# Unread products ahead of 15 waits of a decoder's middle stage, with new lane orders

## The chip, the cores and the metric

The kernel runs on one core of one Trainium2 chip. The metric is the device time of one execution in microseconds; three executions of the kernel before were timed. One further execution was profiled. Engines are named as in the profile: PE (TensorE), DVE (VectorE), ACT (ScalarE), POOL (GpSimd), SP (SyncE).

## The reference, cut to what matters

The reference is a decoder of four layers on x of 16 x 256 tokens of width 128, each layer an attention, a cross attention and a feed-forward part, each with a residual and a layer norm. The middle stage of the kernel computes the last of these of layer 0 (the quantised feed-forward's down projection and its norm), then layer 1's segment attention, cross attention and the gate of its experts:

```python
x = _layernorm(x + _L0_ffn_ref(x, ...))          # lead lane: down projection, norm
x = _layernorm(x + _L1_attn_ref(x, ...))         # near lane
x = _layernorm(x + _L1_xattn_ref(x, ctx_1024, ...))   # far lane
x = _layernorm(x + _L1_ffn_ref(x, ...))          # far lane: gate; then the experts
...
# _L1_attn_ref: 16 heads of 8, segments of 64 tokens
out = _attn(q, k, v)                             # inside the segment
kd = k[:, :, :, dil_idx, :]                      # every 4th key
for off in range(1, NN + 1):                     # two neighbours on each side
    for sign in (-1, 1):
        cross = _attn(q, kd[:, nc], vd[:, nc])
        out = out + jnp.where(valid, cross * w, 0.0)
return out @ Wo + bo
```

The last stage computes layers 2 and 3 from the gated convolution on.

## The kernel before

The 4096 tokens are worked on in eight groups of 512 (`ITERS` = 8), features on the 128 partitions. The program runs stages one after the other: the first stage (layer 0's recurrence and cross attention), the quantised up projection, the middle stage, the choice and the experts of layer 1, the ends, the convolution, and the last stage.

**Lanes.** Each stage is written as lanes: Python generators, one for each engine, that issue a step's instructions and then yield. The middle stage has three. *Lead* (`LaneDown`, then a `LaneNorm`) takes group it+1, *near* (`LaneSegment`, then a `LaneNorm`) takes group it, *far* (`LaneWide`, `LaneNorm`, `LaneGate`) takes group it-1. Near uses one half of PSUM (four banks), lead and far share the other half, one after the other. `middle` runs lead for group 0 alone, then near 0 with lead 1 (`ORDERS["alone"]`), then six steady rounds (`ORDERS["middle"]`: near against far followed by lead), then near 7 with far 6 (`ORDERS["closing"]`), then far 7 alone.

**What sets the order.** `turns` goes through a string for each engine: at "n" it takes the next step of the near lane, at "f" of the other. So a string fixes the order of instructions in an engine's queue; engines execute their queues in order, and semaphores (`wait_ge`, `then_inc`) tie them to each other. The last stage has two equal lanes with strings of its own for its four rounds.

**The near lane's steps on PE** (`LaneSegment.pe`): the projections q, k, v (L1181 to L1191); for each half b of the group the local part: scores (L1208), peaks (transposes of the maxima, L1168), turned (L1222), out in two halves (L1233), back (L1244); then for each half the dilated part: dil_scores (L1257), dil_peaks (L1168), dil_turned (L1270), dil_out (L1279), dil_sum (L920 and L1292); then the output products z (L920 and L939) and the norm's transposes (L1021). Between them DVE searches the maxima (L1368, L1388), makes the query (L1340) and normalises (L1378 to L1407), and ACT takes the exponentials (L1318, L1328). The norm: DVE statistics (L991, L996), POOL's reciprocal root (L1007, L1009), DVE scaling (L1000), PE transposes (L1021), ACT copies (L1032). The lead lane quantises on DVE (L210 to L214) before its product (L1127). The far lane: q (L1454), k and v (L1464), folded output weights (L1477), scores (L1485, L1489), transposes first and second (L1514), out (L920, L1522), gate (L1638).

**Unread products.** `keep_busy(pe, bank, place)` issues as many products of the 128 x 128 identity with itself as `BUSY` names for the place, into a bank whose contents nobody reads any more; for a place that `BUSY` doesn't name it issues nothing. Before the change `BUSY` names only places of the choice and of the experts, whose products are L2801 in the profile. `LaneSegment.pause` calls it for the near lane with a bank of the other lane while that lane's flag `beside["free"]` is set; none of its places is in `BUSY`.

Of the kernel before, what the change touches and what calls it, by code (L numbers as in the profile page):

```python
# [27 lines left out]
P = 128  # L28
# [696 lines left out]
class Convolution:  # L725
# [54 lines left out]
    def dve(self, dve, n):  # L780
        m, i = self.mem, n % 4
        dve.wait_ge(*self.sig.done("pe", f"c{n}", 0))
        if n >= 2:
# [9 lines left out]
BUSY = {'taken': 20, 'chosen': 5, 'choice start': 8, 'choice same': 4, 'choice bit': 3, 'choice rank': 40}  # L793
# [13 lines left out]
        "pe": "nffnnnnnfnnnnnnnnnffffnnnnnnnnnnnnnnnn",  # L807
        "dve": "fnnnfnnnnffffnnnnfnnnnnnnnnnnnnn",
        "act": "nnnnnnnnnnnnnnfffffnnnnnfnnnnn",
# [3 lines left out]
        "pe": "nffnfnfnfnnnfnfffnnfnnfnnffnfnnnfffffnnfffnfnnnfffnnnfnnnn",  # L813
        "dve": "nffnfnffnnnffnffnffnnnfnnffffffnnfffnnfnfffffnnnnnnn",
        "act": "nffffnnnnfffffnnnnnffffnnnnffffffnnnnnnnffffffnnfn",
# [3 lines left out]
        "pe": "nffnfnfnfnnnnfffnfnfnnfnfnfnfnnnnfffnffnnnnnnnnnnn",  # L819
        "dve": "nffnfnffnnnffnfnfffnnnfnnfffffnnfnnnfnnfnnnnn",  # L820
        "act": "fnfffnnnnfffffnnnnnffffnnnnnnffffnnnffnnnnn",
# [9 lines left out]
        "pe": "nnffnnnfnnnnnffffffnfnnfnnfnffnfnfnnnfnnffnffnffffnnnnnnnnnnffffnfffffffnnnnnnnnnfffnfffffffnnfnfnfnfnffnnfffffnfnnffnff"  # L831
             "nnnnfnnffnffnnfnfnnnnnnffnnfnnnffffffnfnfnnnfnfffnfnnfnnfnnfnfnfffffnnnnnnnffffnfffnfnfnfnfnfnfnfnfnfnfnfnfnfnfnfnfnfnfn"
             "fnfnfnnfnfnfnfnfnfnfnfnnffnnnnfnnnfnfffffffnnnnnnnnfnnnfffffffffffnnnnnnnnnnnnfffffnnnnnnnnnnfffnnnnffffffnfnfnffnnnfnnf"
             "nfnfnnnnnffffnffnfnffnfnnffnnfnnffnnnnfnnnfnnnnfffnnnnnnnnnfnfnnffnfnffnfnfnnnnfffnffffffffnnnfffffnfffnnfnnfnnnfnfffnfn"
             "nfffnnnnnnnfffnfnffnnfnffnfffnnnnnnfffnnfnffnnnnnnnfffffnffnnffnnfffnfnfnfnfffnfffnfnfffnffffnfnfnfnfnnfnfnfnfnfnfnfnfnf"
             "nfnfnfffnfnnnfnnnfnnnnffnnnnfnfnnnnfnfnfffffffnnnnnffffffnnfnnnfffffffnnfnnfffnnnnffffffnnnnffnnnnffffffnnffffffffnfffnn"
             "fffnnnnfffnnffffnfnnfnfnfffnfnnnfnnnnfnnnnfnfffnnfnnfnnnfnnnnfffnfnnfffnfnfnffnnnnffffffffnffnnfnfnfnnffnfffnnnfnfnffnnf"
             "nnfnnffnnnnnffnnnnnfffnnfnnnnffffffnnfnnnfnnnffnfnnnfnnnnfnffnfnfnfnffnfnffnfnffnnffffnfnffnfnfnfnfnfnfnfnfnfnnfnfnfnfnf"
             "nfnnffnnnnfnnnnnfnfnnnnnnnfnnnnfffffnnnnnnfnnnnnnnnnnnnnnnnffnnnnnnffnnnfnfnfnnffffffnfnnfffnnfnffffnfffnnnnnnnnffffffnf"
             "fnnnnfnfnnfffnfffnnnfffffnnnnnfnnnnfffnfnnffnnfffnnnnfffffnnnfnffnnfnfnnfnfnfnfnfnfnfffnfnnffffnnfffffffnnnnnffffffnfffn"  # L840
             "fffnnffnfffnfffffnfffffnffnfnnfnnfnffnffffnnnnnnffnfnffnnfnfnffnffnfnfnffffnfnffnnfffffffnfnfnfnfnfnfnfnfnfnfnfnfnfnfnfn"
             "fnfnffnnnffnnnnffnnnffnnnnnnnnfnfnnffffffnnnnnffnffnnnfnffnfnnffffnnfffffffnnnnfffffnfnffffffffnffffffffnnnnffff",
        "dve": "nnffnnnfffnnfnnfnfffnnnnnnffffffnnnnnnfffnfffnfnfnnfnnnffnfffnnfnfffnnffnnfffnnffffnfnnffnnnnffnfnfnfnnnfnnffnnnfnnffffn"
             "nfnfffnnnnnfffnfffnnnnnnnfffffnfffnnfnffnnffnnffnnffnnffnnffnnffnnffnnnnnffnfnfnffffnnnnnnnnffnfffnfffnnfnnnnnffffnnnnnn"
             "nnnfnfffnnnnnffnfffffnnnnnnnffnfnnnnnnfffnffnnnfnnfffffnnffnnffnffnfffnnffnnfnnnnfnnnffnnfnnnfnfnfnnfnfffffnnnffnnffnfff"
             "nnnfnnnfnfnfffnfnfnffnfffnfffnfffffnfffnfnffnnffnnffnnffnfnfnnnnfnnfnnffnnnnnfnnnfnffffffnfnfnnfffffffffnnnnffffnnfffnnf"
             "nnnfffffnnfnffffnnnnnfffnfffnnnnnnnnnfffnnnffnfnfnffnnfnffffnnfffnfnnffnnnffnfnnnfnfnnffnnnnfnfnfnnnfnnffnnfnfffnnnfnfnf"
             "ffnffnnnnnnnffnfnnnffffffnnfffffnffnfnfnffnnffnnffnnffnnfnnnnfnnnnfnnnfnnnnnfnfnnnnnnnnffnnnnnnnfffffnnfnffnnnnnffffnfff"
             "fnnnnnfnnnffnffnnnnnnffnnffnnnfffffnnffnnffnnfnnnnfffnffnnfnnnnfffnffnffnnfnfffnfnfffnnffnfffnnnfffnnfffffffnfffffffnnnf"
             "nnfnnfffnfnfnnfffnfffnfffnnffffffffnfnffnnffnnffnnffnnffnnnfnfnnnnffnnnnffnnnnfnfnfnffnnffffffffffffffffnnnnffff",  # L850
        "act": "nnnfffnnnnnfffffnnnnnfffffnnnnnnnnfffffnffffnnnnnnffffffnnnnnnffffnnffffnnffnnfffffnnfffnnnnnfnffffnnfnnnfnnnnnfffffnnnn"
             "nfffffnnnnnnnnfffffnffffnnnnnnnfffffffnnnnffffnnnnffffnnnnffffnnnnffffnnnnffffnnnnffffnnnnffffnnnnfffnnnnfffffnnnnnnnnff"
             "ffffffnnnnnnnnnnnnnnnnffffnnfffnnffnfnnfffnnfnnnfffnnfnnnnnfffffffnnnnnffnnnffnfnnnfffnnnffnnnnnnnnffffffffnnfnnnnffffff"
             "nnnnfffnnffffnnnfnnffnnnffnnffffnnnnnfffffffnnnnfnnnnfnnnnnnnnfffffnnnfffnffnnnnfffffffffnnnnfffffffnnnnffffnnnnffffnnnn"
             "ffffnnnnffffnnnfffnfnnnnfffnnnnfnnnnfffffffffffnnnnfnnnnfffnfnffnnffnnnnffffnnfffffnnnfnnffnnffffffffffffnnnfnnfffffnnnn"
             "nfffffnnnnnnnnnfffffnnnfffnnnfnnffnfnffnnfnnnnffffffffnnnnnffnffnnnfffnnnfnffnnfnnfnnnfffnnnnfnfnnnnnffnfnnfnfnnnnnnnfff"
             "ffnnnnffffffnnnffnfnnnffnfffffnnnnffffnnnnffffnnnnffffnnnnffffnnnnnnnnfffnnnnfnnnnffffnnnnnfffnnnnnnnnnnnnnfnnnnnnnfffnn"
             "fnnnffffnnnnffnffffffnnnnnnnnnffffffffnnnffnnnfffffffnnfnnnnnnfffffffnnfffffnnnnnnffffnnfnnnnnfffffnfnfffffffffnnnnnffff"
             "ffffnnnnnfffffffffffnnnnfnffffnnnfnnnnnnffnnfffnnnnfffffnnnnfffffffffnnnnfffffffnnnnffffnnnnffffnnnnffffnnnnffffnnnfffnf"
             "nnnnffffnnnnnnnnffffffffnnnnnfffnnnnnfnnnffffffffnnffffnnfnfffffffffffffnnnfff",  # L860
        "pool": "nfnfnnffnnnnnnnnnnnnffffffffffffnnnnffffnnnfffnnnnnnnnnnnnnnnnffffffffffffffffnnnnnnnnnnnnffffffffffffnnffnnnnnnnnnnnnnn"
             "nnnnnnnnnnnnnnnnnnnnnfffffffffffffffffffffffffffffffffffnnnnnfffffnnnnnnnnnnnnnfffffffffffffnnnnnnnnnnnnnnnnnnnfffffffff"
             "ffffffffffnnnnnnnnnnnnnnnnnnnnnnnnnnnnffffffffffffffffnnffffffffffffffnnnnnnnnnnnnnnnnnnnnnnnnnnnnnnnnnnnnnnnnffffffffff"
             "ffffffffffffffffffffffffffffffnnnnnnnnnnffffffffnffnnfffnnnnnnnnnnnnnnnnffffffffffffnnnfffffffnnnnnnnnnnnnnnnnffffffffff"
             "ffffffnnnnnnnnnnnnnnffffffffffffffnnnnnnnnnnnnnnnnnnnnnnnnnnnnnnnnnnnnnnnnnnnnnnnnnnnnnfffffffffffffffffffffffffffffffff"
             "fffffffnnnnnnnnnnnnnnnnffffffffnnnfffffffffffffffffnnnnnnnnnnnnnnnnfffffffnnnnnnnnnnnnffffffffffffffnnffffffffffffffffnn"
# [106 lines left out]
class LaneNorm:  # L973
# [38 lines left out]
    def pe(self, pe, n, meanwhile=None):  # L1012
        m, sg = self.lane, self.sig
        yield
        if meanwhile is not None:
            meanwhile()
        yield
        for (half, _, tiles), bank in zip(HALVES, (0, 1)):
            pe.wait_ge(*sg.done("dve", f"scaled{tiles[-1]}", n))
            for k, i in enumerate(tiles):  # L1020
                mm = pe.transpose(m.bank[:, bank, k * P:(k + 1) * P], m.xs[:, i, :], m.ident)  # L1021
            mm.then_inc(*sg.up("pe", half + "features"))
            yield
# [118 lines left out]
class LaneSegment:  # L1142
# [28 lines left out]
    def pause(self, pe, place):  # L1171

        if self.lane.beside["free"]:
            self.lane.keep_busy(pe, self.lane.beside["bank"], place)

    def pe(self, pe, n, x_ready):
# [18 lines left out]
        for b in range(G):  # L1195
            self.pause(pe, f"scores{b}")
            if b:
                pe.wait_ge(*sg.done("dve", f"norm{b - 1}", n))
            else:
                pe.wait_ge(*sg.done("act", "v1", n))  # L1200
                pe.wait_ge(*sg.done("dve", f"vd{G - 1}", n))
                m.carry_product(pe, bank)
# [9 lines left out]
            self.pause(pe, f"peaks{b}")  # L1212
# [3 lines left out]
            self.pause(pe, f"turned{b}")  # L1216
# [10 lines left out]
            self.pause(pe, f"out{b}")  # L1227
            for half, step in enumerate(("first_exp", "exp")):
                pe.wait_ge(*sg.done("act", f"{step}{b}", n))
# [10 lines left out]
            self.pause(pe, f"back{b}")  # L1240
# [7 lines left out]
        for b in range(G):  # L1248
            self.pause(pe, f"dil_scores{b}")
# [11 lines left out]
            self.pause(pe, f"dil_peaks{b}")  # L1261
# [3 lines left out]
            self.pause(pe, f"dil_turned{b}")  # L1265
# [8 lines left out]
            self.pause(pe, f"dil_out{b}")  # L1274
# [11 lines left out]
            self.pause(pe, f"dil_sum{b}")  # L1286
# [8 lines left out]
        for b, (half, _, tiles) in enumerate(HALVES):  # L1295
            pe.wait_ge(*sg.done("act", f"middle{b}", n))
# [121 lines left out]
class LaneWide:  # L1418
# [26 lines left out]
    def pe(self, pe, n, x_ready):  # L1445
        m, sg, w = self.lane, self.sig, self.w
        bank, beside = m.bank, m.beside
        beside["free"], beside["bank"] = False, bank[:, 2, :]
# [45 lines left out]
        beside["free"] = True  # L1494
# [9 lines left out]
        for u in range(NT):  # L1504
            m.keep_busy(pe, bank[:, 2, :], f"first{u}")
            beside["free"] = False
# [9 lines left out]
            yield  # L1516
            pe.wait_ge(*sg.done("act", f"copy1_{u}", n))
# [809 lines left out]
class SelfLayer:  # L2327
# [65 lines left out]
    def pe(self, pe, n, x_ready, biased_ready):  # L2393
# [11 lines left out]
        for k, (b, j) in enumerate(self.ORDER):  # L2405
            if b == 0:
                pe.wait_ge(*sg.done("dve", f"keys{j}", n))
            if k:
                pe.wait_ge(*sg.done("act", f"copied{k - 1}", n))
# [1299 lines left out]
```

## Time and profile before

| | us |
|---|---|
| three runs, median (lowest to highest) | 3095.99 (3090.25 to 3096.03) |
| the profiled execution, its time | 3092.62 |
| its span, first to last instruction | 3090.8 |
| mean granted clock of TensorE | 0.87 |
| near lane alone with lead (358.0 to 448.7) | 90.7 |
| six steady rounds (448.7 to 1097.0) | 648.3 |
| closing round (1097.0 to 1200.5) | 103.5 |
| far lane alone (1200.5 to 1265.0) | 64.5 |
| last stage, from about 1600 | 1490.8 |

A round is counted from the start of one q projection of the near lane (L1181) to that of the next. The granted clock is given as a share of full speed: 1.00 is 2.4 GHz and 0.50 is 1.2 GHz, and a mean between them tells how the time was divided between the two.

### The profile page before, as it was taken

The page shows a single profiled execution, that of the slowest core. Times are in us where ns is not written, and L with a number is a line of the kernel's source. Part 1 is how long each engine was busy: PE and PEld are TensorE (multiplying, and loading weights), DVE is VectorE, ACT ScalarE, POOL GpSimd, SP SyncE. Part 2 cuts the span into 40 slices and gives each one's busy share as a digit, 9 for nine tenths or more (in the row PEclk, how much of TensorE's full clock was granted, in tenths as well). Part 3 has the DMA queues.
Part 4 walks back from the last instruction along what each step waited for, and adds up shares of the span by engine and source line. Part 5 has one row for each costly group of instructions (what it writes and reads, how often), then busy time and mean ns, then how long its engine had stood idle before and what let it go on. Part 6 is the DMA issues. An engine that isn't in the chain of part 4 may idle for free.

```text
span 3090.8 us, 47481 instructions
## 1 busy us (share of the span) xinstructions
PE 2391.3 (77%) x20196; PEld 1589.6 (51%) x20196; DVE 1694.6 (55%) x4103; ACT 1040.4 (34%) x1534; POOL 357.9 (12%) x605
## 2 busy tenths in 40 slices
PE   4665478887888887787678779777797777887788
PEld 2433256666666665665545454444454444544444
DVE  5776736556665663531358651675417753447641
ACT  4464212222322231012132542434423344334442
POOL 0111000011001000036111000110001100111000
PEclk9887568878978887988788999899898899999999
DMA  2000000000000000212710000000000000000000
GB/s 89 1 1 3 1 1 8 1 8 8 8 1 8 8 1 8 102 24 34 175 64 1 1 8 1 1 1 1 8 0 1 1 1 4 4 1 1 1 1 28
DMA packets 39335, 47.80 MB, mean 15 GB/s; under 512 B 7170, under 2 KB 36370, under 8 KB 38355
## 3 DMA queue, kind: packets, MB, share of 16 engines
q1 hardware_dynamic: 33490, 40.43, 4.4%
q0 software_dynamic: 5632, 4.33, 1.1%
q8 instruction: 159, 2.61, 0.4%
q14 instruction: 54, 0.43, 0.0%
HBM read 31.82 MB, written 12.91 MB: 14 GB/s over the span
## 4 chain that ended last, share of the span: by engine, by line
PE 57%; DVE 25%; ACT 8%; issue 4%; POOL 3%; DMA 1%; SPq 0%; DVEq 0%; another core or an unknown queue 0%; POOLq 0%; ACTq 0%
PE banks L2604 7%; DVE wide_area L2477 4%; PE banks L1279 3%; PE banks L1489 2%; DVE wide_area L1891 2%; PE banks L920 2%; PE banks L2353 2%; PE banks L1454 2%; PE banks L1522 2%; PE banks L2362 2%; PE banks L948 2%; PE banks L2372 2%; PE banks L1802 1%; PE banks L1788 1%; PE banks L2591 1%
## 5 line engine op out<-in xcount | busy, mean ns | idle before, releaser
L2477 DVE TENSOR_REDUCE wide_area<-banks 128x8 f32<-128x2048 f32 x64 | 146.7, 2292 | 106.2 <-PE banks L2353 106.0
L2456 ACT ACTIVATE weights<-banks 128x2048 f32<-128x2048 f32 x64 | 120.0, 1877 | 128.4 <-PE banks L2362 128.3
L1007 POOL TENSOR_TENSOR rstd<-moments,eps 128x4 f32<-128x4 f32 x56 | 11.9, 212 | 1208.5 <-DVE moments L996 1208.5
L991 DVE BATCH_NORM_STATS2 stats<-banks 128x6 f32<-128x128 f32 x208 | 50.3, 287 | 181.3 <-PE banks L959 100.1
L1891 DVE TENSOR_REDUCE wide_area<-banks 128x16 f32<-128x1024 f32 x80 | 94.3, 1217 | 44.3 <-PE banks L1788 44.2
L1279 PE MATMUL banks<-wC,weights 128*128 128x72 f32 x512 | 84.7, 343 | 18.3 <-ACT weights L1328 18.3
L991 DVE BATCH_NORM_STATS2 dilvals<-banks 128x6 f32<-128x128 f32 x144 | 35.2, 287 | 113.6 <-PE banks L959 85.0
L1279 PEld LDWEIGHTS banks<-wC,weights 128*128 128x128 f32 x512 | 81.8, 255 | 26.3 <-ACT weights L1328 26.3
L1021 PE MATMUL banks<-wA,xs 128*128 128x128 f32 x208 | 49.2, 335 | 59.1 <-DVE xs L1000 58.2
L1000 DVE TENSOR_SCALAR xs<-banks,moments,rstd 128x128 f32<-128x128 f32 x208 | 70.6, 401 | 37.0 <-POOL rstd L1009 36.8
L2604 PE MATMUL banks<-wide_area,big 128*128 128x512 f32 x192 | 87.0, 595 | 0.0
L2266 DVE TENSOR_TENSOR weights<-banks,wC 128x1024 f32<-128x1024 f32 x64 | 76.1, 1215 | 15.5 <-PE banks L2131 15.3
L1856 ACT ACTIVATE weights<-banks 128x1024 f32<-128x1024 f32 x64 | 62.1, 1021 | 65.9 <-PE banks L1802 65.8
L1596 DVE TENSOR_REDUCE smalls<-banks 128x16 f32<-128x1024 f32 x32 | 39.1, 1223 | 77.3 <-PE banks L1489 77.3
L1489 PE MATMUL banks<-gates,wide_area 128*128 128x128 f32 x512 | 77.5, 296 | 0.0
L1007 POOL TENSOR_TENSOR smalls<-smalls,eps 128x4 f32<-128x4 f32 x16 | 3.2, 201 | 637.0 <-DVE smalls L996 637.0
L1489 PEld LDWEIGHTS banks<-gates,wide_area 128*128 128x128 f32 x512 | 65.0, 199 | 16.4 <-issue 16.4
L1032 ACT ACTIVATE xf<-banks 128x256 f32<-128x256 f32 x64 | 24.0, 383 | 132.2 <-PE banks L1021 131.8
L1021 PEld LDWEIGHTS banks<-wA,xs 128*128 128x128 f32 x208 | 25.4, 160 | 81.7 <-DVE xs L1000 76.0
L2414 PE MATMUL banks<-wA,wide_area 128*128 128x128 f32 x128 | 28.5, 306 | 49.2 <-DVE wide_area L2477 49.0
L1000 DVE TENSOR_SCALAR gates<-banks,dilvals 128x128 f32<-128x128 f32 x144 | 49.1, 402 | 28.4 <-POOL dilvals L1009 28.3
L1328 ACT ACTIVATE weights<-banks 128x1024 f32<-128x1024 f32 x32 | 31.0, 1021 | 98.1 <-PE banks L1270 98.1
(776 smaller groups left out, 6273.0 us busy)
## 6 DMA issues: line engine op xcount, KB each, us to landing
big<-in_wE SPq DMA_DIRECT2D x1, 4096.0 KB, 12.8
weights<-long_kernel SPq DMA_DIRECT2D x8, 512.0 KB, 7.5
conv<-wide_area SPq DMA_DIRECT2D x16, 256.0 KB, 3.0
wC<-in_wC SPq DMA_DIRECT2D x1, 3012.0 KB, 17.3
wC<-in_wG SPq DMA_DIRECT2D x1, 2971.0 KB, 19.3
big<-in_wT SPq DMA_DIRECT2D x1, 2560.0 KB, 11.3
x_all<-in_xT SPq DMA_DIRECT2D x1, 2048.0 KB, 10.9
total<-spread SPq DMA_DIRECT2D x8, 256.0 KB, 2.3
```

The lines of the kernel that those rows point to most:

```text
L920: pe.matmul(out, x, ident, start=True, stop=False, is_transpose=True)
L991: dve.bn_stats(m.stats[:, i, :], self.tokens(i)).then_inc(*sg.up("dve", f"stats{i}"))
L1000: dve.tensor_scalar(m.xs[:, i, :], self.tokens(i), m.moments[:, i, 0:1], m.rstd[:, i:i + 1], ALU.subtract, ALU.mult).then_inc(*sg.up("dve" ...
L1021: mm = pe.transpose(m.bank[:, bank, k * P:(k + 1) * P], m.xs[:, i, :], m.ident)
L1279: mm = pe.matmul(bank[:, 2 * half + i, c % 4 * self.BLOCK:(c % 4 + 1) * self.BLOCK], m.weights[:, c * S + i * P:c * S + (i + 1) * P], m.di ...
L1489: mm = pe.matmul(bank[:, i, (p % 4) * P:(p % 4 + 1) * P], m.wide_q[:, p, u * P:(u + 1) * P], m.wide_k[:, p, u // 2, :, :].rearrange("p j k ...
L1856: act.activation(m.weights[:, part], wide[:, part], ACT.Exp, scale=DK ** -0.5).then_inc(*sg.up("act", f"{step}{b}"))
L1891: dve.tensor_reduce(m.peaks[:, p, :, :].rearrange("p i (r c) -> p r i c", r=4)[:, :, :, at:at + 2], bank[:, :, :].rearrange("p r (i j k) - ...
L2266: dve.tensor_tensor(m.weights[:, half * 1024:half * 1024 + 1024].rearrange("p (h q) -> p h q", h=H // 2), bank[:, 2 * half:2 * half + 2, : ...
L2456: act.activation(m.weights, bank[:, :, :].rearrange("p r c -> p (r c)"), ACT.Exp, scale=DK ** -0.5)\
L2477: return dve.tensor_reduce(m.peaks[:, k % 2, :, :].rearrange("p t (r c) -> p r t c", r=4)[:, :, :, SPARE[j]], m.bank[:, :, :].rearrange("p ...
L2604: mm = pe.matmul(m.bank[:, self.BANKS[name][c], :], w[name][:, k * FF + c * P:k * FF + (c + 1) * P], src[k], start=(k == 0), stop=(k == FC ...
```

## The change

- `BUSY` gets 15 new places: three on the lead lane, nine on the near lane, three on the far lane, with 1 to 14 products each, 61 in a steady round.
- `keep_busy` is now called by `LaneNorm.pe` ahead of its transposes into bank 0; `LaneSegment.pause` takes a bank of the near lane itself, and the flag `beside` goes. Ahead of dil_sum the PE queue first waits for `dil_part1`, so that bank 1 has been read. Calls that `BUSY` doesn't name, those in the last stage's classes among them, issue nothing.
- The strings for "alone", "middle", "closing" and "last" are other ones. Of their letters differ in the middle round: PE 8 of 58, DVE 2 of 52, ACT 6 of 50, POOL none; alone: PE 8 of 38, DVE 6 of 32, ACT 12 of 30; closing: PE 10 of 50, DVE 10 of 45, ACT 6 of 43; last: PE 390 of 1432, DVE 136 of 952, ACT 184 of 1158, POOL 14 of 818.

```diff
-BUSY = {'taken': 20, 'chosen': 5, 'choice start': 8, 'choice same': 4, 'choice bit': 3, 'choice rank': 40}
+BUSY = {'lead z': 2, 'lead norm': 10, 'lead product': 10, 'back0': 4, 'back1': 1, 'dil_scores0': 1, 'dil_turned0': 2, 'dil_sum0': 2, 'dil_scores1': 3, 'dil_turned1': 1, 'dil_sum1': 2, 'near norm': 14, 'first3': 3, 'far norm': 1, 'gate': 5, 'taken': 20, 'chosen': 5, 'choice start': 8, 'choice same': 4, 'choice bit': 3, 'choice rank': 40}
...
     "middle": {
-        "pe": "nffnfnfnfnnnfnfffnnfnnfnnffnfnnnfffffnnfffnfnnnfffnnnfnnnn",
-        "dve": "nffnfnffnnnffnffnffnnnfnnffffffnnfffnnfnfffffnnnnnnn",
-        "act": "nffffnnnnfffffnnnnnffffnnnnffffffnnnnnnnffffffnnfn",
+        "pe": "nffnfnfnfnnnfnffnfnfnnfnfnfnnfnnfffffnnfffnnfnnfffnnnfnnnn",
+        "dve": "nffnfnffnnnffnfnfffnnnfnnffffffnnfffnnfnfffffnnnnnnn",
+        "act": "fnffnnnfnfffffnnnnnffffnnnnffffffnnnnnnnfffffffnnn",
...
@@ LaneNorm.pe
+        m.keep_busy(pe, m.bank[:, 0, :], f"{m.name} norm")
         for (half, _, tiles), bank in zip(HALVES, (0, 1)):
             pe.wait_ge(*sg.done("dve", f"scaled{tiles[-1]}", n))
...
@@ LaneSegment
-    def pause(self, pe, place):
-
-        if self.lane.beside["free"]:
-            self.lane.keep_busy(pe, self.lane.beside["bank"], place)
+    def pause(self, pe, bank, place):
+        self.lane.keep_busy(pe, self.lane.bank[:, bank, :], place)
...
-            self.pause(pe, f"back{b}")
+            self.pause(pe, 1, f"back{b}")
             pe.wait_ge(*sg.done("act", f"copied{b}", n))
...
-            self.pause(pe, f"dil_scores{b}")
+            self.pause(pe, 2, f"dil_scores{b}")
...
-            self.pause(pe, f"dil_turned{b}")
+            self.pause(pe, 1, f"dil_turned{b}")
             pe.wait_ge(*sg.done("dve", f"dil_query1_{b}", n))
...
-            self.pause(pe, f"dil_sum{b}")
+            pe.wait_ge(*sg.done("dve", f"dil_part1_{b}", n))
+            self.pause(pe, 1, f"dil_sum{b}")
             pe.wait_ge(*sg.done("dve", f"dil_part3_{b}", n))
...
@@ LaneWide.pe
-            beside["free"] = False
```

## Rows read from the trace of the kernel before

**Rows 1.** The page: granted clock in 40 slices, and the chain by engine.

```profile
PEclk9887568878978887988788999899898899999999
...
PE 57%; DVE 25%; ACT 8%; issue 4%; POOL 3%; DMA 1%; SPq 0%; DVEq 0%; another core or an unknown queue 0%; POOLq 0%; ACTq 0%
```

**Rows 2.** Stretches: length, busy us of PE, PEld, DVE, ACT, POOL; PEclk, DMA share, GB/s.

```profile
358.00:448.70 90.70, 57.53 (x566) 44.99 (x566) 33.27 (x72) 15.49 (x23) 3.93 (x8) 0.59 0.00 1
...
667.60:773.20 105.60, 86.99 (x866) 67.27 (x866) 64.30 (x120) 29.00 (x46) 9.35 (x20) 0.86 0.02 6
...
773.20:882.10 108.90, 90.56 (x865) 70.34 (x865) 64.30 (x120) 29.04 (x46) 9.35 (x20) 0.81 0.02 6
...
1097.00:1200.50 103.50, 83.07 (x854) 64.86 (x855) 57.41 (x103) 28.32 (x45) 7.54 (x17) 0.86 0.02 6
...
1600.00:3090.80 1490.80, 1207.75 (x9569) 722.63 (x9568) 809.40 (x2004) 580.49 (x821) 140.28 (x246) 0.94 0.01 3
```

**Rows 3.** The same view, cut where the granted clock changes.

```profile
757.50:767.80 10.30, 7.90 (x38) 7.50 (x38) 3.16 (x8) 0.90 (x3) 0.00 (x0) 0.50 0.00 0
...
778.00:819.00 41.00, 36.59 (x457) 27.66 (x459) 30.27 (x42) 15.21 (x22) 0.00 (x0) 1.00 0.01 2
...
819.00:825.80 6.80, 6.80 (x67) 6.02 (x63) 2.29 (x3) 1.94 (x2) 0.00 (x0) 0.50 0.01 2
...
825.80:849.70 23.90, 18.77 (x217) 15.89 (x218) 14.62 (x32) 6.53 (x10) 3.87 (x7) 1.00 0.07 21
...
849.70:877.00 27.30, 21.86 (x109) 17.79 (x109) 13.86 (x33) 3.69 (x8) 2.81 (x7) 0.50 0.02 3
...
880.40:887.20 6.80, 6.33 (x34) 3.00 (x36) 1.76 (x4) 1.67 (x4) 0.57 (x2) 0.50 0.00 0
```

**Rows 4.** The chain of waits of one round: start us, us, engine, tile, line.

```profile
796.16 1.94 PE banks L1222 x64
...
821.83 3.41 PE banks L1522 x16
...
838.84 1.79 PE banks L1522 x16
...
840.62 1.12 PE banks L1270 x16
...
842.84 3.81 PE banks L1279 x32
...
857.07 1.13 PE banks L1168 x4
...
859.14 2.13 PE banks L1270 x16
...
862.38 7.12 PE banks L1279 x32
...
872.78 0.85 PE banks L1292 x4
...
882.13 2.07 PE banks L1181 x2
```

**Rows 5.** Timeline of DVE: start us, us, line, operation, tiles, idle time before.

```profile
850.62 1.81 DVE L210 TENSOR_SCALAR weights<-big,hscale 128x1536 f32<-128x1536 f32 x1
...
854.65 2.35 DVE L1388 TENSOR_REDUCE spread<-banks 128x64 f32<-128x1024 f32 x2 [0.24 <-PE banks L1257]
```

**Rows 6.** Timeline of PE in the experts: unread products of the kernel before.

```profile
1355.16 1.28 PE L2801 MATMUL banks<-wA 128*128 128x128 f32 x10
```

**Rows 7.** Timeline of PE in the round of rows 3: waits.

```profile
818.30 3.12 PE L1222 MATMUL banks<-spread,keys 32*128 32x64 f32 x64 [1.15 <-DVE spread L1340]
...
849.51 0.34 PE L920 MATMUL banks<-wA,heads 128*128 128x128 f32 x1 [0.85 <-DVE spread L1407]
...
872.31 0.47 PE L920 MATMUL banks<-wA,heads 128*128 128x128 f32 x1 [2.40 <-DVE spread L1407]
...
880.33 1.32 PE L1021 MATMUL banks<-wA,xs 128*128 128x128 f32 x4 [2.91 <-DVE xs L1000]
```

## What the change does to the time: the prediction, made before the changed kernel ran

> **What bounds the kernel now.** I read the page first. TensorE carries 57% of the chain that ended last, DVE 25%, and the granted clock of TensorE is far from even: in the slices of the middle stage (about the 6th to the 16th of 40) it moves between 5 and 9 tenths [rows 1]. The table of stretches then gives each round of the middle stage: the six steady rounds take from 105.6 to 109.9 us, 648.3 together (448.7 to 1097.0; two of them are shown), at a mean clock of 0.80 to 0.86, and the last stage runs at 0.94 [rows 2]. The reader should see that TensorE is not full in these rounds (87.0 of 105.6 and 90.6 of 108.9 us); it is slow in places, and waits in others.
>
> Third, one round cut at the instants at which the clock changes. From 778.0 to 819.0 it is 1.00 (2.4 GHz), from 819.0 to 825.8 it is 0.50 (1.2 GHz), then 1.00, then 0.50 from 849.7 to 877.0, 1.00 for 3.4 us, and 0.50 again for 6.8 us; in the shorter kind of round a part of the long stretch is at 1.00 and pieces such as 757.5 to 767.8 are at 0.50 [rows 3]. So a round of the longer kind has 41 us at half clock. What the engine did before each fall: before 819.0 it waited 1.15 us for the query, with groups of four short transposes ahead of that; before 849.7 it ran the tiny gate products and waited 0.85 us; before 880.4 it waited 2.91 us for the normalised tokens [rows 7].
>
> Fourth, whether that time is on the path. The chain of waits of the same round runs from 842 to 887 us through the near lane alone, one step after another: products, DVE maximum, transposes, DVE query, products, exponentials, products. The far lane has nothing left to put beside it. The same product group stands there at both clocks: L1279 (32 products) 3.81 and 7.12 us, L1270 1.12 and 2.13 us, L1222 1.94 and 3.12 us, L1522 1.79 and 3.41 us [rows 4].
>
> **The change, part by part.**
>
> (a) *Products that nobody reads*, 61 in a steady round (2+10+10 on the lead lane, 4+1+1+2+2+3+1+2+14 on the near lane, 3+1+5 on the far lane). One costs about 0.11 us at full clock: ten such products of the expert stage take 1.28 us with the drain of the last [rows 6]. At half clock it is 0.21 us, from four equal products in 0.85 us [rows 4]. So 6.5 us of TensorE work per round at full clock, 13 at half. What covers them: the 14 ahead of the near norm (1.5 us) lie in the wait of 2.91 us, the 10 of the lead norm and 2 of dil_sum1 in the wait of 2.40 us, the others in waits like those of 0.85 and 1.15 us [rows 7]. Ahead of a DVE peak search of 2.35 us [rows 5] stand the 10 of the lead product. If such a wait shrinks, its products come onto the path; I put 1.5 us per round down for that, as I can't show that each of the 15 fits.
>
> What they buy, for the longer round of [rows 4], if the clock stays at 1.00. Second dilated pass: L1270 2.13 to 1.12 (1.0), L1279 7.12 to 3.81 (3.3), the transposes before the query 1.13 halved (0.5), dil_sum1 with its ten products of 0.21 us halved (1.1), the twelve z products of the same kind (1.25). After the norm: q, k and a part of v, from 882.1 [rows 4] to the rise at 887.2 (5.1 halved, 2.5), and the transposes ahead of them 0.3, together 2.8. The dil_scores1 products (2.1 to 1.1) and dil_sum0 before them give almost nothing: DVE is busy from 850.62 with the three quantising passes of the lead lane and starts the peak search at 854.65 after only 0.24 us of idle time [rows 5]. What is late next there is DVE, so I take 0.2. Sum 10.2 us. In 819.0 to 825.8: L1222 1.2, L1522 1.6, the scores 0.2, together 3.0.
>
> (b) *Order of the middle stage.* Decoding the letters: on TensorE, peaks1 goes ahead of first/second1, dil_turned0 ahead of out3, dil_turned1 ahead of the lead z, dil_scores0 ahead of out2; on DVE query1 goes ahead of soft2. The first pair removes most of the 1.15 us wait before L1222 [rows 7], because the transposes of the far lane now run while DVE makes the query; soft2 becomes 0.9 us later, and its reader is behind turned1, out1 and scores3, so it has time. I take 0.8 us. The same swap puts L1222 nearer to the transposes, which closes the thin place before 819.0 even though no unread product stands there. dil_turned0 earlier by 1 us makes out3, the far norm and DVE's far scaling later by as much, and DVE does that scaling before dil_recip0: I take zero, bounds -1 to +1 us.
>
> (c) *The added wait*: dil_part1 before the products of dil_sum. The two later parts are 0.7 us after it on DVE, and TensorE would have waited for dil_part3 anyway; behind it in TensorE's queue stand only dil_sum and what waits for it. Zero. The removed flags and the places of the old pause issued nothing.
>
> (d) *Sum for the middle stage.* A round at full clock: 108.9 - 10.2 - 3.0 - 0.8 = 94.9 us. As all six rounds do the same work, 648.3 - 6 x 94.9 = 79 us. The round with the near lane alone (90.7 us at 0.59) and the closing one (103.5 us at 0.86) [rows 2] have the same second pass: 7.4 us each plus some 2 of the products behind it, 9 each by estimate, 18. Together 97. Off that: 8 x 1.5 = 12 for products that stick out, and 10 for places where the clock falls all the same (choice; one to two falls of the 3 us kind for every second round). 75 us remain.
>
> (e) *Last stage*, 1491 us. No unread products go in there; 390 of 1432 letters of TensorE's order differ, 136 of 952 of DVE's, 184 of 1158 of ACT's. The trace of before can't show the new order. At 0.94 some 12% of the stage, 180 us, runs at half clock, worth at most 90 us; a new order shifts a tenth of it, and single waits of about 1 us as in (b), either way. I take 0, bounds -12 to +12 us.
>
> The profiled execution took 3092.6 us (span 3090.8), 3.4 below the median of 3096.0 and 2.3 above the lowest. 3092.6 - 75 = 3017.6, and I say 3018.
>
> The Trainium skill bears on one point. The rows say that the clock fell at 819.0 with no idle time longer than 1.15 us before it [rows 3, 7], so it follows how full TensorE is, not one gap. The Trainium skill, "TensorE: Matmul & The Clock Gate", section "Why this matters for your kernels", advises against long idle gaps between bursts of products. By that rule alone 14 of the 15 places would be useless; the trace disagrees with it as the whole story.
>
> **The rivals.**
>
> *Half of it.* Several places get 1 to 3 products, 0.1 to 0.3 us. If the clock still falls once in the second dilated pass, a round keeps L1279 at 7.1 or the part from dil_sum1 on: the shorter rounds of before are such a case, 3.3 us better than the longer. Then only 5 to 7 us per round come, 40 to 50 in all: 3048. For it: the counts are thin. Against: one full pass of L1279 plus filled waits is denser than stretches that held 1.00, such as 825.8 to 849.7 [rows 3].
>
> *Only the long gap counts.* Products ahead of the near norm keep the clock for q, k and v (2.8 us), the rest does nothing: 8 x 2.8 = 22, so 3070. Against: the fall at 819.0. It is the rule of the Trainium skill named above.
>
> *It does nothing*: the clock falls where it did and the products hide: 3093.
>
> *Slower.* The unread products do not lift the clock, so each takes 0.21 us. Lead product: 2.1 plus 1.5 for its own products, against 2.4 of peak search, 1.2 over. Lead norm with dil_sum1: 2.1 + 0.4 + 0.5 against 2.8, 0.2 to 0.4 over; near norm 3.0 against 2.9, 0.1; lead z and turned 0.4. Two to 2.5 us per round, 8 rounds, 20 us: 3113. It decides as soon as TensorE stays at 1.2 GHz in the second dilated pass. Against it: TensorE held 1.00 over 825.8 to 849.7 while busy 18.8 of 23.9 us with gaps of its own [rows 3].
>
> **How the numbers follow.** Forecast 0.57 (3018); half 0.22 (3048); long gap only 0.08 (3070); nothing 0.06 (3093); slower 0.07 (3113). The forecast's own range is 2984 (the whole 97 us and 12 from the last stage) to 3040 (a stage that loses 12 and some more products that stick out); with the half case the range for 8 in 10 is 2984 to 3056. A measurement of this kernel can tell about 0.2%, 6 us, from no change. Faster: 0.57 + 0.22 + 0.08 and a little of the rest, 0.88; same 0.05; slower 0.07.
>
> **What would show it.** The clock row of the page at 9 in the slices of the middle stage; rounds near 95 us at a clock over 0.95; L1279 at 3.8 us in both passes of each round; L1222 in its second use near 2 us with a wait under 0.5 us; DVE's peak search of dil_scores1 still right behind the quantising passes; near-norm wait with some 1.5 us of products in it. Wrong would be: L1279 still at 7 us in most rounds, the three half-clock stretches in place, or a last stage that moved by over 12 us.

## The result, and the profile after

The changed kernel took 3051.0 us (median of four runs, 3046.8 to 3053.1). Four runs of the kernel before have a median of 3093.1 us, with one at 3082.4. The recorded ratio is 0.989, with a 95% interval of 0.9865 to 0.9915: 1.1% faster, which is 34 us; the two medians are 42 us apart. The forecast was 3018 us, a gain of 75, so about half of it came. In a later series, with both kernels on one chip, the ratio was 0.9907 (0.9886 to 0.9929), which is 29 us.

The page of the changed kernel, its clock row and its row of unread products (out<-in, count, busy, mean ns, idle before):

```profile
PEclk8887679999999998997998999979899889999999
...
L2805 PE MATMUL banks<-wA 128*128 128x128 f32 x1290 | 192.2, 297 | 6.0 <-DVE spread L1406 6.0
```

The steady rounds (444 to 1055 us) are now at 9, where [rows 1] had 7 to 9 in them; ahead of them, with the near lane alone, the clock still stands at 6 and 7. The count of the unread products is more than twice what one expects: 1290 records, 956 more than the 334 of the kernel before, in eight rounds. That is 119 a round, and `BUSY` names 61.

The stretches that answer to [rows 2] (columns as there): the near lane alone, two steady rounds, the last stage:

```profile
357.00:443.90 86.90, 64.95 (x669) 55.46 (x669) 34.48 (x72) 15.49 (x24) 3.93 (x8) 0.73 0.00 1
...
545.50:647.10 101.60, 91.43 (x988) 74.95 (x988) 64.09 (x120) 28.94 (x47) 9.48 (x20) 0.97 0.02 7
...
749.50:851.90 102.40, 92.23 (x988) 75.54 (x988) 64.08 (x120) 28.91 (x47) 9.48 (x20) 0.95 0.03 7
...
1501.00:3051.10 1550.10, 1244.14 (x9824) 744.73 (x9824) 830.79 (x2064) 601.30 (x849) 145.80 (x265) 0.93 0.02 6
```

A steady round takes 100.9 to 102.5 us instead of 105.6 to 109.9, and not the 94.9 of the forecast. From the first near q product to the choice's first product, the middle stage went from 911.9 to 871.1 us, 41 less. Cut from its first product on, the last stage went from 1536.7 to 1550.1 us, 13 more. What lies between the two has the same instructions and took 284.3 and 273.0 us; this difference can't be put down to the change. In the profiles of the later series it took 271.0 to 276.4 us on one chip (seven kernels) and 282.6 to 289.4 on another (four).

The round of 749.5 cut where its clock changes, as in [rows 3]:

```profile
749.50:773.70 24.20, 22.47 (x262) 15.93 (x262) 14.59 (x24) 7.99 (x13) 0.00 (x0) 1.00 0.01 2
773.70:783.90 10.20, 8.64 (x90) 7.15 (x91) 2.45 (x2) 3.04 (x5) 0.00 (x0) 0.50 0.01 2
783.90:851.90 68.00, 61.12 (x638) 52.47 (x637) 47.04 (x94) 17.88 (x31) 9.48 (x20) 1.00 0.04 9
```

In this round the half-clock places of [rows 3] are gone, the second dilated pass among them, and there is a new one from 773.7 to 783.9, where the kernel before ran at full clock. The timelines of PE and then of ACT show what happens there (start, length, idle time and its releaser in brackets):

```profile
770.21 2.01 PE L1220 MATMUL banks<-spread,keys 32*128 32x64 f32 x64
775.26 0.60 PE L1483 MATMUL banks<-kmask_g,vals 2*128 2x512 bf16 x1 [3.04 <-ACT value_area L1544]
775.79 2.08 PE L1487 MATMUL banks<-gates,wide_area 128*128 128x128 f32 x8
```

```profile
772.29 1.94 ACT L1317 ACTIVATE weights<-banks 128x1024 f32<-128x1024 f32 x2 [6.55 <-PE banks L1220]
774.11 1.09 ACT L1544 ACTIVATE value_area<-banks 128x512 f32<-128x512 f32 x2
```

TensorE waits 3.04 us, from 772.2 to 775.26, for ACT's two copies of the folded output weights (L1544). ACT had been idle for 6.55 us, waiting for turned0, with the copies queued behind the exponentials of exps0 (L1317). The products that they copy (L1475) had been done for about 4 us when ACT went on. In the kernel before, the copies stood in front. This is a step of ACT's order string, and the first suspect.

### The profile page after: what moved, and what is told of

Read it like the earlier page. It is cut to its first block, busy times and chain, and to the rows that moved or that the text cites. A ratio compares the mean times of both kernels' runs of the same rounds, so it can differ in the third digit from the quotient of the medians.

```text
span 3051.2 us, 49389 instructions
## 1 busy us (share of the span) xinstructions
PE 2415.3 (79%) x21152; PEld 1644.0 (54%) x21152; DVE 1689.6 (55%) x4103; ACT 1041.1 (34%) x1536; POOL 357.5 (12%) x605
## 4 chain that ended last, share of the span: by engine, by line
PE 58%; DVE 24%; ACT 9%; issue 4%; POOL 4%; DMA 1%; SPq 0%; DVEq 0%; ACTq 0%; POOLq 0%
PE banks L2608 7%; DVE wide_area L2481 4%; PE banks L1487 3%; PE banks L2805 2%; DVE wide_area L1891 2%; PE banks L2355 2%; PE banks L1452 2%; PE banks L1518 2%; PE banks L920 2%; PE banks L2364 2%; PE banks L1799 2%; PE banks L2595 2%; PE banks L2374 2%; PE banks L1784 2%; PE banks L948 2%
## 5 line engine op out<-in xcount | busy, mean ns | idle before, releaser
L2805 PE MATMUL banks<-wA 128*128 128x128 f32 x1290 | 192.2, 297 | 6.0 <-DVE spread L1406 6.0
L2805 PEld LDWEIGHTS banks<-wA 128*128 128x128 f32 x1290 | 171.9, 208 | 16.0 <-issue 8.7
L1487 PE MATMUL banks<-gates,wide_area 128*128 128x128 f32 x512 | 87.3, 322 | 0.0
L1856 ACT ACTIVATE weights<-banks 128x1024 f32<-128x1024 f32 x64 | 62.4, 1021 | 70.4 <-PE banks L1799 70.2
L1487 PEld LDWEIGHTS banks<-gates,wide_area 128*128 128x128 f32 x512 | 73.5, 221 | 17.1 <-issue 17.1
L1007 POOL TENSOR_TENSOR smalls<-smalls,eps 128x4 f32<-128x4 f32 x16 | 3.2, 199 | 656.4 <-DVE smalls L996 656.4
L1276 PE MATMUL banks<-wC,weights 128*128 128x72 f32 x512 | 66.4, 293 | 5.0 <-ACT weights L1327 4.6
L1276 PEld LDWEIGHTS banks<-wC,weights 128*128 128x128 f32 x512 | 64.6, 208 | 8.3 <-ACT weights L1327 8.3
```

The costliest lines, as they stand in the source:

```text
L1276: mm = pe.matmul(bank[:, 2 * half + i, c % 4 * self.BLOCK:(c % 4 + 1) * self.BLOCK], m.weights[:, c * S + i * P:c * S + (i + 1) * P], m.di ...
L1487: mm = pe.matmul(bank[:, i, (p % 4) * P:(p % 4 + 1) * P], m.wide_q[:, p, u * P:(u + 1) * P], m.wide_k[:, p, u // 2, :, :].rearrange("p j k ...
L1856: act.activation(m.weights[:, part], wide[:, part], ACT.Exp, scale=DK ** -0.5).then_inc(*sg.up("act", f"{step}{b}"))
L2805: pe.matmul(bank[:, 0:P], m.ident, m.ident, start=True, stop=True)
```

## The experiments

Ratios are to the kernel before, run on the same chip in the same series, with 95% intervals. Most expectations give absolute times that start from 3051 and 3093 us. On the chip of experiments 1 to 5, 9 and 10 the kernel before took 3082.4 and 3080.7 us, on the chip of experiments 6 to 8 it took 3089.2 us. So a time that lies inside such a range says less than the ratio and the rounds.

### 1. ACT's copies ahead of exps0

```diff
     "middle": {
-        "act": "fnffnnnfnfffffnnnnnffffnnnnffffffnnnnnnnfffffffnnn",
+        "act": "fnfffnnnnfffffnnnnnffffnnnnffffffnnnnnnnfffffffnnn",
     "closing": {
-        "act": "fnffnnnfnfffffnnnnnffffnnnnnnffffnnnnnffnnn",
+        "act": "fnfffnnnnfffffnnnnnffffnnnnnnffffnnnnnffnnn",
```

> The changed kernel (3051.0 us) with one step of ACT moved back in the middle and closing rounds: the two copies of the folded output weights (value_area, L1544) ahead of exps0 (L1317) again; all else as changed. Theory A: this one step of ACT's order costs 7 us in each round, the 3.04 us in which TensorE waits for L1544 and the fall of the clock to 0.50 for 10.2 us that follows it; so a steady round goes from 102.4 to about 95 us, the wait at L1483 is gone, and the kernel takes 3051 - 7 x 6.5 = 3005 us (3000 to 3012). Rival B: the round is long because 61 unread products of 0.21 us each stick out (13 us); the wait at L1483 is only where the slack shows, and without it the time moves by under 10 us: 3041 to 3051.

Measured: 3008.9 us, 0.9761 (0.9730 to 0.9791). Steady rounds in its stretches, and the place in its timeline of PE and ACT:

```profile
635.60:731.00 95.40, 88.24 (x988) 72.25 (x988) 64.18 (x120) 29.03 (x47) 9.50 (x20) 1.00 0.03 7
731.00:826.40 95.40, 88.24 (x988) 72.23 (x988) 64.18 (x120) 29.02 (x47) 9.50 (x20) 1.00 0.03 7
```

```profile
749.62 1.09 ACT L1544 ACTIVATE value_area<-banks 128x512 f32<-128x512 f32 x2 [2.38 <-PE banks L1475]
753.79 1.94 ACT L1317 ACTIVATE weights<-banks 128x1024 f32<-128x1024 f32 x2 [3.08 <-PE banks L1220]
```

```profile
753.55 0.38 PE L1483 MATMUL banks<-kmask_g,vals 2*128 2x512 bf16 x1
753.85 1.16 PE L1487 MATMUL banks<-gates,wide_area 128*128 128x128 f32 x8
```

This moves one step of 50 in one string. The copies now run in a gap of ACT that was there anyway, TensorE goes on without a wait, and all six steady rounds take 95.4 to 95.6 us with no half clock at all. From the end of turned0 to the end of back0 TensorE takes 5.3 us (753.7 to 759.0) where the changed kernel takes 12.4 (772.2 to 784.6). 3.0 of the 7.1 us are the wait itself; most of the others are the same products at half clock, as L1487 with 2.08 and 1.16 us. Theory A stands; rival B, that the unread products make the length, falls, since they are all still in. By the ratios the step is worth 40 us (0.989 to 0.9761) or 45 (0.9907 to 0.9761), where theory A had 46.

### 2. and 3. The last stage's order of before; both edits

> The changed kernel with the order strings of the last stage of the kernel before; the middle stage as changed. Theory A: the new order of the last stage loses what the two profiled executions show, 1550.2 against 1536.6 us from the first gated product to the end, so this gives 3051 - 13.6 = 3037 us (3033 to 3042). Rival B: the 13.6 us are the spread of one execution against another and the order brings nothing either way: 3051, within 4. The middle stage stays at 871 us from the first q projection to the first product of the choice.

Measured: 3040.8 us, 0.9860 (0.9833 to 0.9886). The time lies in theory A's range, but 0.9860 of 3093 is 3050 us, which is rival B's. The middle stage took 876.6 us, not the 871 expected.

> Both of these edits together: copies ahead of exps0 and the last stage's order of before. Theory A: the two are apart in time and add up, 3051 - 46 - 14 = 2991 us (2985 to 3000). Rival B of both: 3040 to 3051. If one of the two turns out wrong, its share is missing here too.

Measured: 3002.6 us, 0.9736 (0.9706 to 0.9766); rounds of 95.4 us. That is above theory A's range of 2985 to 3000 us. On the same chip it is 6.4 us less than experiment 1, within the spread of the two. The sign is that of theory A in both pairs, the size is not settled by them: 0.989 or 0.9907 to 0.9860 would be 9 or 14 us, 0.9761 to 0.9736 8 us. Hence the next one.

### 4. The new last stage alone, in the kernel before

The kernel before, with only the strings of `ORDERS["last"]` taken from the changed one.

> The kernel before with nothing changed but the last stage's order strings, which are those of the changed kernel. Theory A: that order costs about 10 us by itself (the last stage of six profiled executions with it averaged 1549 us, of four with the old one 1538 us): 1.003 of the kernel before, 1.002 to 1.005. Rival B: the difference comes from when the last stage begins, after a shorter middle stage, and not from the order: 1.000, within 0.001.

Measured: 3097.2 us, 1.0052 (1.0035 to 1.0070): 16 us slower, 11 to 22 by the interval, a little beyond theory A's 1.002 to 1.005. Its last stage:

```profile
1542.50:3095.40 1552.90, 1248.73 (x9824) 749.83 (x9824) 830.07 (x2064) 601.24 (x849) 145.70 (x265) 0.93 0.02 6
```

The changed kernel itself ran once more in another series, for the spread of this stage:

> The changed kernel itself, once more beside the others, as their yardstick on one chip. On this chip the kernel before may stand near 3082 us as in the last series; by the ratio of 0.989 the changed one then takes about 3048 us. The last stage of its profiled execution tells how much that stage varies with one and the same order: Theory A (the new order costs 10 us or more) expects 1546 us or more again, rival B (spread of executions) anything from 1531 to 1550 us.

Measured: 3061.3 us, 0.9907 (0.9886 to 0.9929), last stage 1544.9 us, just under the 1546 of theory A and inside rival B's range. Over eight profiled executions with the new order the stage took 1533.7 to 1554.4 us, 1547.7 in the mean; over five with the old one 1530.7 to 1548.2, 1538.9 in the mean. On the one chip that has both, the means are 1543.1 (three executions) and 1539.5 (four). The ranges overlap, so the profiles don't decide this. The timed ratio of 1.0052 does, and it is for theory A.

In experiment 4 the middle stage in front of it is that of before (913.1 us), so the loss belongs to the order and not to a shorter middle stage. Behind the new middle stage the order's price came out smaller, 6 to 14 us (experiments 2 and 3). Which of its changed letters make it, no run shows.

### 5. The unread products with all old orders

The changed kernel's code and `BUSY`; every string of before.

> The changed kernel's code and BUSY (61 unread products in a round) with every order string of the kernel before. Theory A: the products raise the clock and that is the gain; the old ACT order has the copies in front, so this is faster than the changed kernel: 8 rounds between 95 and 99 us instead of 102.4 and 14 us from the last stage, 3005 to 3025 us. Rival B: the counts only fit the new orders (the query ahead of soft2, the transposes of the far lane behind peaks1), and with the old ones the clock still falls at turned1 and in the second dilated pass: rounds of 103 us and more, 3045 to 3080.

Measured: 3030.7 us, 0.9831 (0.9800 to 0.9862), a little behind the range of theory A. This is faster than the changed kernel (0.989 and 0.9907): taken together, the new orders made the products worth less. Rounds of 104.1, 102.4, 102.5 us and then 99.3, 99.2, 99.2: not the 95.4 of experiment 1, and only the first in the 103 and more of rival B. The timeline of PE in the round of 656.4 shows why:

```profile
699.38 2.01 PE L1220 MATMUL banks<-spread,keys 32*128 32x64 f32 x64 [1.15 <-DVE spread L1339]
...
723.64 5.53 PE L1276 MATMUL banks<-wC,weights 128*128 128x72 f32 x32 [1.14 <-ACT weights L1327]
```

The wait of 1.15 us for the query is there as before, and the clock still falls for 3.4 us or more behind it and, in the first three rounds, for 6.8 us over dil_out0. With the new orders both falls are gone (experiment 1). So the new middle orders are worth some 4 to 9 us a round, apart from the one step of ACT that takes 5 to 7 us away again.

### 6. The orders without the products

Experiment 1 with the `BUSY` of the kernel before.

> The kernel of e1_copies_first without the 61 unread products of the middle stage (its BUSY is that of the kernel before); orders as in e1, where a steady round took 95.4 us at full clock throughout. Theory A: the products are what holds the clock; without them the half-clock stretches of the kernel before return in the second dilated pass and behind the near norm, 10 us a round, and the order alone gives the rest: rounds of 104 to 107 us, 3009 + 6 x 10 + 8 = 3077 us (3065 to 3085). Rival B: the order gives most of the gain and the clock is secondary: rounds of 97 to 100 us, 3020 to 3040.

Measured: 3091.6 us, 1.0005 (0.9990 to 1.0019). One of its rounds, and a stretch inside another:

```profile
764.90:870.60 105.70, 89.48 (x866) 68.68 (x866) 64.35 (x120) 29.02 (x47) 9.49 (x20) 0.82 0.02 6
...
733.90:761.20 27.30, 20.96 (x103) 16.28 (x101) 14.12 (x37) 3.85 (x8) 2.81 (x7) 0.50 0.04 11
```

The products are what holds the clock in the second dilated pass: without them the rounds take 103.4 to 106.0 us and that pass is back at 0.50. With the same orders TensorE is busy for 89.5 us in such a round, and for 88.2 with the 61 products in it: their 13.6 us (61 times 0.223, see experiment 7) are paid for by the other products, which run at full clock, and the round is 8 to 10.6 us shorter.

One of the places of [rows 3] doesn't come back, the fall behind the wait for the query. The timeline of PE in the round of 764.9 has no idle time there any more, and the group takes 2.01 us instead of 3.12:

```profile
808.17 2.01 PE L1220 MATMUL banks<-spread,keys 32*128 32x64 f32 x64
```

It is so in all six rounds. In experiment 5, with the products and the old orders, the clock falls there in all six. So at this place the order alone did it, by taking the wait away, and in the second dilated pass the products did. The orders' own gain, some 3 us a round and 14 over the middle stage (911.9 to 897.9), is about what the new last stage takes away, hence a ratio of 1. The 3091.6 us are above theory A's 3065 to 3085; this chip is also 7 us slower with the kernel before.

### 7. The price of one product

```diff
-'near norm': 14
+'near norm': 28
```

> The kernel of e1_copies_first with 28 instead of 14 unread products ahead of the near norm. A product is two matmul records of 0.107 us. Theory A: 14 fill the wait for the normalised tokens to the brim, so each further one is on the path with 0.213 us: 14 x 0.213 = 3.0 us a round, 8 rounds, 24 us more than e1 (3033). Rival B, the price that the prediction used: 0.107 us each, of which a part is still hidden: 0 to 1.5 us a round, at most 12 us (3009 to 3021).

Measured: 3046.8 us, 0.9860 (0.9839 to 0.9881), on the chip of the second series. Its timeline of PE ahead of the norm's transposes, and a round:

```profile
736.84 6.42 PE L2805 MATMUL banks<-wA 128*128 128x128 f32 x56
743.09 0.60 PE L1022 MATMUL banks<-wA,xs 128*128 128x128 f32 x4
```

```profile
546.60:644.80 98.20, 91.11 (x1016) 75.35 (x1016) 64.17 (x120) 28.88 (x47) 9.49 (x20) 1.00 0.03 7
```

28 products are 56 records, and 56 records take 6.25 us from the first to the transposes behind them: 0.223 us a product at full clock. A round is 98.2 to 98.4 us where no half clock falls in, 2.8 to 3.0 us more than 95.4; 14 times 0.223 is 3.1, so each product above 14 is on the path with nearly its whole length. That is theory A for the price. The middle stage grew by 20.7 us (832.1 to 852.8); the whole time grew by more, 31 us by the ratios, and the rest lies outside of what was changed. The 14 of the change fill the wait to the brim: in the changed kernel the first transposes start right behind them, and the second still wait 0.20 us for DVE's scaled tokens.

### 8. The closing round

```diff
+            if b and isinstance(n, int) and n == ITERS - 1:
+                m.keep_busy(pe, m.other_bank[:, 3, :], "closing peaks")
             pe.wait_ge(*sg.done("dve", f"dil_max1_{b}", n))
```

`BUSY` names 10 for the place.

> The kernel of e1_copies_first, and in the closing round alone 10 unread products more, ahead of the wait for the second dilated peak search, in a bank of the other lane that is idle there. In e1 the closing round still ran 20.5 us at half clock from 1095.4 on. Theory A: the closing round got nothing from the change because the 20 products of the lead lane are not in it; with 10 of them the clock stays up, L1268 and L1276 of the second pass go from 2.1 and 7.1 to 1.1 and 3.8 us, and the time falls by 5 to 7 us. Rival B: the clock there falls for the wait of 1.68 us ahead of dil_sum0 and would stay down; no change within 2 us.

Measured: 3018.7 us, 0.9769 (0.9745 to 0.9792). The stretch from the last near q product to the choice, first in experiment 1, then here:

```profile
1017.30:1190.00 172.70, 145.11 (x1267) 117.94 (x1268) 88.65 (x158) 43.54 (x68) 12.49 (x28) 0.87 0.04 10
```

```profile
1018.40:1183.90 165.50, 140.09 (x1286) 113.57 (x1287) 88.82 (x158) 43.52 (x68) 12.46 (x28) 0.92 0.04 10
```

The stretch lost 7.2 us and the fall of 20.5 us is gone (L1278, the dil_out of this kernel, is back at 3.79 us), so the mechanism is as theory A has it. The whole time does not show it: 0.9769 against 0.9761, on two chips. In the profiles the part between the choice and the last stage is 9 us longer here, and the last stage 8.

### 9. Half of the products

Experiment 1 with every middle-stage count halved and rounded down, 27 in place of 61.

> The kernel of e1_copies_first (3008.9 us, steady rounds of 95.4 us without half clock) with every count of unread products of the middle stage halved and rounded down, 27 in place of 61 in a round. Theory A: the counts are near what the clock needs, and the thin places (1 to 3 products) fall to nothing; the clock falls again in the second dilated pass or behind the norm in most rounds, rounds of 98 to 103 us, 3030 to 3055 us. Rival B: half of them would do, and what is left out comes off the path: rounds of 93 to 95.4 us, 2995 to 3009 us.

Measured: 3022.8 us, 0.9832 (0.9808 to 0.9857). Two rounds and a fall in the second:

```profile
642.50:740.70 98.20, 85.61 (x920) 67.10 (x920) 64.08 (x120) 29.09 (x47) 9.47 (x20) 0.97 0.03 7
740.70:840.40 99.70, 88.14 (x920) 70.30 (x920) 64.17 (x120) 28.99 (x47) 9.48 (x20) 0.93 0.03 7
818.40:832.10 13.70, 12.74 (x67) 11.74 (x66) 5.66 (x21) 1.94 (x2) 1.21 (x2) 0.50 0.01 1
```

Rounds of 97.0 to 99.8 us with falls of 3.4 to 13.7 us: by its rounds theory A, though mildly; its time lies just below that theory's range. Half of the products buys more than half of the gain: with none a round took 105.0 us in the mean, with 27 98.5, with 61 95.4.

### 10. All together

Copies first, 10 products in the closing round, last stage of before.

> All that was found put together: the copies ahead of exps0, the 10 unread products in the closing round, and the last stage's order of before. If the shares add up: e1 stood 0.9761 of the kernel before, the last stage's order brings 6 to 10 us (0.002 to 0.003), the closing round 7 us (0.002): 0.971 to 0.972, on a chip where before takes 3089 us some 3001 us (2992 to 3008). Rival: the closing round's 7 us are lost again behind it, and it stands no better than e3 (0.9736).

Measured: 2998.2 us, 0.9724 (0.9706 to 0.9741), the lowest time of the case: 2.8% under before, 1.7 to 1.8 points better than the changed one. It can't be told apart from experiment 3 (0.9736), so the whole time shows nothing of the products in the closing round. The closing stretch took 169.1 us here, against 172.5 and 172.7 without them; a fall of 10.2 us at 1105.0, that experiment 8 did not have, kept half of the 7 us.

## Why the prediction was right and wrong

**Right: the clock.** Part (a) said that the products would hold the clock in the second dilated pass and behind the near norm, part (b) that a swap in the order would hold it behind the second query, where no product stands, and part (d) that a steady round at full clock would take 94.9 us. Experiment 1 takes 95.4 to 95.6 in every steady round at 1.00. Experiment 6 shows that the products do the first, and experiments 5 and 6 together that the order does the second. In the changed kernel the dil_out group (L1276) of the round shown takes 3.69 and 3.79 us, against 3.81 and 7.12 in [rows 4]. DVE's peak search starts right behind the quantising passes, as (a) read it from [rows 5]:

```profile
728.05 0.96 DVE L214 TENSOR_SCALAR whole_h<-weights 128x1536 bf16<-128x1536 f32 x1
728.93 2.35 DVE L1387 TENSOR_REDUCE spread<-banks 128x64 f32<-128x1024 f32 x2
```

**Wrong: part (b), the order.** This is the step of the prediction that failed. It decoded TensorE's and DVE's strings and passed over ACT's, though the diff shows 6 of 50 changed letters there, and so put ACT's order at nothing without a reason. The step it did not see, exps0 ahead of the copies of the output weights, costs 6.5 us a round in the profiled execution: 3 us of wait, the rest from the clock. That is 39 us of six rounds, more than the whole shortfall of 33 us. In two further executions with the same middle stage (the second series and experiment 2) the falls were shorter, the rounds took 100.2 to 101.6 us, and it was 5.7 a round.

**Wrong: part (e), the last stage.** It was taken as 0 within 12 us either way; by itself it costs 16 (11 to 22), so the bound, made from the half-clock share, was too small or just reached. Taking an unknown order as zero hid a loss.

**Mis-sized: the price of a product.** 0.11 us came from dividing 1.28 us by the 10 of [rows 6]. But that row is `chosen` with 5 products: the profile shows two records for each 128 x 128 f32 product. A product costs 0.223 us at full clock, and at half clock not 0.21 us but 0.43, since the four records in 0.85 us of [rows 4] are two products. [rows 4] would have told too: the loop at L1522 issues 8 products, and the chain counts 16. It did little harm to the forecast: 13.6 us of products a round, and still 95.4 us, 0.5 over the clean sum and 1.0 under the sum with the 1.5 us put down for products that stick out. The rival "slower" reckoned with 0.21 us at half clock; with 0.43 its own sum gives some 10 us a round and 80 in all, by estimate, in place of its 20.

**Wrong: part (d), the two outer rounds.** 9 us were put down for each. The near lane alone won 3.8 (90.7 to 86.9) at a mean clock of only 0.73, and 1.7 to 1.8 in the two further executions; why the clock stays low there, no run shows. The closing stretch won nothing (172.9 to 172.8), and in the two further executions it took 181.1 us, 8 longer than before. ACT's order may have a part in this: with the copies first it took 172.7 and 172.5 us (experiments 1 and 3). 22 of the 61 products stand on the lead lane, and there is no lead in the closing round. Experiment 8 put 10 of them back and got 7.2 us, experiment 10 3.4 to 3.6.

**The sum again.** The forecast gain was 75 us. The measured terms are: six rounds at full clock 75.8 (experiment 1: 572.5 instead of 648.3; forecast 79 before the deductions), outer rounds 4, last stage -16: 64. Less six times 6.5 us for ACT's order, 39, that leaves 25. Measured were 29 us in the series on one chip, 34 by the recorded ratio and 42 by the medians. The two profiled spans differ by 40: 41 from the middle stage, -13 from the last, and 11 from the part between them, which is the same in both. Without those 11 the profiles give 28.

**The rivals.** *Half of it* (3048) is 3 us from the measured time, but that is luck: by its mechanism the clock would still fall in the second dilated pass, and it did not. That the forecast's 3018 us is near the 3009 of experiment 1 says little too, since that run stands beside a kernel before of 3082. *Only the long gap* fell: the second pass is at full clock.

**What goes with a fall of the clock.** The fall that was left in the changed kernel goes with the wait of 3.04 us and is gone without it (experiment 1), in all six rounds. In [rows 3, 7] the clock fell behind waits of 1.15 and 0.85 us, and also behind one of 2.91 us. The Trainium skill ("TensorE: Matmul & The Clock Gate", "Why this matters for your kernels") warns of the long idle gap between bursts of products. The new fall stands at the longest wait of the round, so it agrees, though in four of the six rounds it began before the wait was over, at 773.7 in the round shown; the old falls behind about 1 us show that keeping the gaps short is not enough. The prediction concluded that the clock follows how full TensorE is. Its rows don't show that for whole stretches: TensorE was busy for 36.59 of 41.00 us ahead of the fall at 819.0, and for 18.77 of 23.90 us in the stretch that held 1.00 [rows 3].

**Open.** What in the new last stage costs 16 us, and why less of it shows behind the new middle stage. Also why the falls of the changed kernel are of different lengths: in three executions of its middle stage they lasted 3.4 to 10.2 us at the same place, the steady rounds took 100.2 to 102.5 us, and the stage 871.1, 876.5 and 876.6 us.

## What to carry to other kernels

- When an order is changed, write out every engine's sequence, the idle engine's too. A copy of 1 us on an engine that is idle for two thirds of the time, put behind a step that waits, cost 5 to 7 us a round.
- Unread products pay where one lane's serial chain leaves TensorE thin: here 61 products of 0.22 us, nearly all inside waits, took a round from 103 to 106 us down to 95.4. Fill to the wait's length and not over it (each product above it cost 0.20 to 0.21 us of the round), and in rounds at the edges of a loop look for which lane's products are missing.
- Test orders of separate stages separately: one sum hid a stage that gained 41 us and one that lost 13. With the products alone and all old orders the kernel was faster than the changed one.
- Where an order takes a wait away, no product is needed there: the fall behind the query went with the order alone.

## What the runs showed of the hardware

- A 128 x 128 product of f32 stands as two matmul records and takes 0.223 us at 2.4 GHz (experiment 7) and 0.43 at 1.2 GHz (four records in 0.85 us, [rows 4]); counts in a profile row are records, not products.
- A wait of 3.04 us of TensorE, after a dense stretch (busy 22.47 of 24.20 us), went with 3.4 to 10.2 us at 1.2 GHz in every steady round of three executions. The same eight-record group took 2.08 instead of 1.16 us there; in the round shown the fall cost more than the wait, 4 us against 3.
- With identical instructions and orders, the last stage took 1530.7 to 1548.2 us in profiled executions of the old order, and the part between the choice and the last stage 271 to 276 us on one chip and 283 to 289 on another. A gain of 3 to 7 us, seen in its own stretch, does not show in the whole.
